# Attention block of a four-layer transformer stack: row maxima in four rows of the query stacks, and an attention output that stays by features

## The chip, the cores and the metric

The kernel runs on one core of one Trainium2 chip. The metric is the device time of one execution in microseconds, from its first to its last instruction and what lies around them. Several executions are taken and the median is given.

## The reference, cut to what matters

There are 16 sequences of 256 tokens with 256 features, each with a context of 77 tokens, and four layers:

```
L0: self-attention (rotary, masked), cross-attention, MLP   (each modulated and gated)
L1: cross-attention                                          (modulated)
L2: self-attention, cross-attention, MLP
L3: self-attention (rotary), cross-attention (rotary), MLP
```

An attention block is `softmax(q k^T / 4) v` with 16 heads of 16 features, a projection of the result, and a residual add. All of it is in float32. There are 16 x 7 = 112 attention blocks, 48 self and 64 cross, and 48 MLPs.

## The kernel before, in words

**Order of the work.** A job is one sequence in one layer, 64 jobs in all. Every block of a job is cut into steps (`attention_steps`), and each step belongs to one engine. A planner in Python (`Program.run`) goes through all jobs with the cost of every step (`cost`), the time its DMA takes on the queue (`ISSUE`) and rings of buffers, up to six jobs at a time in six slots. It writes down one fixed order for each engine. On the chip the engines follow their orders, and semaphores hold them where an input isn't there. So a step that comes later than planned holds all that stands behind it on its engine. SP's queue (SyncE) is such an order too: it issues nearly all the DMAs, and waits in front of each for its source.

**Scores.** A head has only 16 features. Queries and keys are split into a high and a low part, and a pair of heads takes a block of 64 rows of 128 partitions. `q_stack` and `k_self`/`k_cross` are filled by DMA through a scratch tensor in DRAM: features 1, 2 and 3 of every four partitions hold parts of the values (`place_high`, `place_low`, steps `lh`, `ll`). Every fourth partition (`0:P:4`, 32 rows) is spare. In the key stacks these rows hold ones or zeros (`hot`), so that what stands in the query stack's rows is added to the scores. The step `zq` (`place_zeros`) fills them with zeros. Then TensorE computes the scores by query (`S`), VectorE their maxima (`mr`, L1637), and `mx` (`negate_maximum`) negates and splits them and turns them in 32x32 blocks, four STREAM_TRANSPOSEs one after the other (L1656). `sd` (`place_maxima`, L1058) writes them by one DMA into all 32 rows of `q_stack`, for each half of the heads. `ST` then computes the scores by key (L1238, L1244) with the maximum already taken off, and ScalarE takes the exponential (`ex`, L1454).

**Output.** `W` (`weigh`, L1263) multiplies values by probabilities. A head's value tile is 17 columns wide, 16 features and a column of ones for the sum of the row. Four heads go side by side into four groups of 32 partitions, two such groups of heads into one bank. `pv` (ScalarE, L1461) copies the bank to `oT`. `oX` (`transpose_back`, L1274) turns it to tokens by four TensorE transposes, `dv` (`divide`, L1665 and L1666) divides by the sums, `atT` (`transpose_output`, L1285) turns it back by four (in a self block two and two), `ae` (L1466) copies it to `atT`, and `out` (`project_out`, through L1146) projects it. `oX`, `dv` and `pv` come once per half of the heads, 224 times.

```
for c in range(TC):
    for i in range(PER_HALF):
        at_col = (c * PER_HALF + i) * P
        mm = pe.transpose(buf[:, at_col:at_col + P], oT[before.buf][:, i, c * P:c * P + P], ident[:, :])
```

## Time and profile before

| | |
|---|---|
| time, median of 3 | 2863.39 us (2859.39 to 2871.44) |
| profiled execution, span | 2855.2 us, 57728 instructions |
| profiled execution, its own time | not listed; a timed execution is 4 to 16 us over this span |
| DMA | 369.43 MB in 278894 packets, mean 129 GB/s |

The span runs from the first to the last instruction of one execution that the hardware profiler recorded. A busy TensorE is not one at its peak: matmuls are pipelined and their ends are modelled. An engine's idle time costs something only where the engine sets the pace. PE is TensorE's matmul, PEld its weight load, DVE is VectorE, ACT ScalarE, POOL GpSimd, SP SyncE; a q behind the name is the engine's DMA queue. L1274 is line 1274 of the kernel. The rows that the prediction uses stand further down.

### The profile page before, as it was taken

What the parts mean: (1) busy time and instruction counts of PE and PEld (TensorE: products, weight loads), DVE (VectorE), ACT (ScalarE), POOL (GpSimd) and SP (SyncE); (2) the same over time, 40 slices, a digit from 0 to 9 for tenths busy, and PEclk for the clock granted to TensorE, in tenths of its full rate; (3) what the DMA queues carried; (4) which work ended last, traced back from release to release, by engine and by line L of the source; (5) the groups of instructions that cost most, each with busy time, mean ns of one, the idle gap of its engine ahead of it and who ended that gap; (6) DMA issues with size and microseconds to landing.
All of it is one profiled execution on the core that took longest, in us unless ns stands there. A gap on an engine that the chain in (4) does not pass through costs nothing.

```text
span 2855.2 us, 57728 instructions
## 1 busy us (share of the span) xinstructions
PE 2716.6 (95%) x21118; PEld 2000.2 (70%) x21118; DVE 1990.0 (70%) x5348; ACT 1433.3 (50%) x2283; POOL 290.6 (10%) x346
## 2 busy tenths in 40 slices
PE   6989999999998999988999999999999999999998
PEld 5657777776766766665777777776777777676766
DVE  4677757766755577776777777776877777787751
ACT  1344554554455455444555555545555555555453
POOL 0000000000001111101111111110100000000000
PEclk9999999999999999997999999999999999999999
DMA  6443343343335366653434444434344433434320
GB/s 199 154 137 116 117 141 106 99 145 109 104 95 149 115 198 191 196 163 122 155 122 139 126 141 125 141 121 131 104 141 138 139 112 107 146 103 145 101 69 14
DMA packets 278894, 369.43 MB, mean 129 GB/s; under 512 B 31130, under 2 KB 157690, under 8 KB 278300
## 3 DMA queue, kind: packets, MB, share of 16 engines
q1 hardware_dynamic: 246172, 318.66, 36.8%
q10 hardware_dynamic: 32256, 47.07, 4.5%
q8 instruction: 177, 2.90, 0.4%
q14 instruction: 97, 0.79, 0.1%
q0 software_dynamic: 192, 0.01, 0.0%
HBM read 224.52 MB, written 110.97 MB: 118 GB/s over the span
## 4 chain that ended last, share of the span: by engine, by line
PE 70%; DVE 16%; issue 5%; DMA 4%; ACT 1%; SPq 1%; POOL 0%; ACTq 0%; DVEq 0%; POOLq 0%
PE gen L1305 11%; PE gen L1314 11%; PE gen L1180 10%; PE gen L1146 8%; PE gen L1263 8%; DVE row_max L1637 6%; PE score L1238 3%; PE score L1193 3%; PE score L1208 3%; PE score L1244 2%; PE gen L1274 2%; PE gen L1155 2%; PE score L1222 2%; DMA parts_scratch<-parts 2%; DVE maxT L1656 2%
## 5 line engine op out<-in xcount | busy, mean ns | idle before, releaser
L1637 DVE TENSOR_REDUCE row_max<-score 128x4 f32<-128x1024 f32 (+1 forms) x640 | 652.6, 1044 | 107.9 <-PE score L1222 88.2
L1454 ACT ACTIVATE probs<-score 128x1024 f32<-128x1024 f32 (+1 forms) x576 | 566.2, 1022 | 268.2 <-PE score L1238 170.3
L1305 PE MATMUL gen<-xnT,w_w1M 128*128 128x256 f32 x1536 | 378.4, 394 | 4.7 <-ACT xnT L1396 2.6
L1314 PE MATMUL gen<-w_w2M,hT 128*128 128x256 f32 x1536 | 354.8, 385 | 8.6 <-DVE x L1688 5.7
L1490 POOL TENSOR_TENSOR rstd<-var_eps,minus_half 128x2 f32<-128x2 f32 x160 | 111.5, 697 | 2175.1 <-DVE var_eps L1533 2175.1
L1314 PEld LDWEIGHTS gen<-w_w2M,hT 128*128 128x128 f32 x1536 | 286.2, 191 | 59.2 <-issue 22.3
L1305 PEld LDWEIGHTS gen<-xnT,w_w1M 128*128 128x128 f32 x1536 | 286.1, 194 | 58.8 <-issue 4.9
L1480 ACT ACTIVATE hT<-gen,b_b 128x256 f32<-128x256 f32 x384 | 160.2, 471 | 166.6 <-PE gen L1305 165.7
L1396 ACT ACTIVATE xnT<-gen,mod_all 128x256 f32<-128x256 f32 x288 | 147.0, 564 | 181.0 <-PE gen L1155 164.4
L1656 DVE STREAM_TRANSPOSE maxT<-max_tok 32x64 f32<-32x64 f32 x896 | 208.9, 233 | 17.1
L1461 ACT COPY oT<-gen 128x512 f32<-128x512 f32 x224 | 131.6, 587 | 171.4 <-PE gen L1263 168.9
L1208 PE MATMUL score<-k_self,q_stack 64*128 64x256 f32 x1536 | 195.7, 343 | 19.7 <-DVE row_max L1637 17.3
L1263 PE MATMUL gen<-probs,v_self 128*17 128x256 f32 x3072 | 201.8, 383 | 0.3 <-ACT probs L1454 0.3
L1686 DVE TENSOR_TENSOR xhat<-gen,gate 128x256 f32<-128x256 f32 (+1 forms) x112 | 60.2, 537 | 203.2 <-PE gen L1314 147.8
L1208 PEld LDWEIGHTS score<-k_self,q_stack 64*128 64x128 f32 x1536 | 128.1, 190 | 95.9 <-issue 77.0
L1238 PE MATMUL score<-q_stack,k_self 64*128 64x256 f32 x1536 | 181.2, 334 | 2.9 <-ACT probs L1454 2.2
L1222 PEld LDWEIGHTS score<-k_cross,q_stack 64*128 64x128 f32 x2048 | 137.5, 192 | 50.6 <-issue 49.5
L1238 PEld LDWEIGHTS score<-q_stack,k_self 64*128 64x128 f32 x1536 | 122.1, 188 | 64.5 <-issue 46.0
L1222 PE MATMUL score<-k_cross,q_stack 64*128 64x78 f32 x2048 | 156.3, 284 | 9.1 <-DVE row_max L1637 5.8
L1263 PE MATMUL gen<-probs,v_cross 77*17 77x256 f32 x2048 | 159.7, 402 | 4.9 <-DVE xhat L1666 1.9
L1665 DVE RECIPROCAL row_max<-gen 128x16 f32<-128x16 f32 x224 | 55.0, 246 | 133.1 <-PE gen L1274 132.9
L1274 PE MATMUL gen<-ident,oT 128*128 128x128 f32 x896 | 143.2, 284 | 0.0
(162 smaller groups left out, 4166.4 us busy)
## 6 DMA issues: line engine op xcount, KB each, us to landing
q_stack<-parts_scratch SPq DMA_DIRECT2D x336, 256.0 KB, 3.8
parts_scratch<-parts ACTq DMA_DIRECT2D x160, 256.0 KB, 2.6
parts_scratch<-parts SPq DMA_DIRECT2D x160, 256.0 KB, 2.9
k_self<-parts_scratch SPq DMA_DIRECT2D x144, 256.0 KB, 4.0
q_stack<-zeros_scratch SPq DMA_DIRECT2D x112, 256.0 KB, 3.9
q_stack<-maxT SPq DMA_DIRECT2D x224, 128.0 KB, 2.6
k_cross<-parts_scratch SPq DMA_DIRECT2D x192, 78.0 KB, 2.5
x_scratch<-x SPq DMA_DIRECT2D x48, 256.0 KB, 3.1
```

The costliest lines, as they stand in the source:

```text
L1146: mm = pe.matmul(out, xT[:, fc], weight[:, fc, cols], start=fc == 0, stop=fc == FC - 1)
L1180: mm = pe.matmul(out[:, c, :], weight[:, fc, cols], xT[:, fc, :], start=fc == 0, stop=fc == FC - 1)
L1208: mm = pe.matmul(buf[:, t, c * S:c * S + S], queries[rows, column(u), c * P:c * P + P], keys[rows, column(u), :], start=not blk.mask, stop ...
L1222: mm = pe.matmul(buf[:, t, at_col:at_col + CTXP], queries[rows, column(2 * u + i), c * P:c * P + P], keys[rows, column(2 * u + i), :], sta ...
L1238: mm = pe.matmul(buf[:, t, kc * S:kc * S + S], keys[rows, column(u), kc * P:kc * P + P], queries[rows, column(u), :], start=not blk.mask, ...
L1263: mm = pe.matmul(pv[VW * i:VW * i + VC, within, :], value, e, start=kc == 0, stop=not blk.whole or kc == TC - 1, skip_group_check=True)
L1274: mm = pe.transpose(buf[:, at_col:at_col + P], oT[before.buf][:, i, c * P:c * P + P], ident[:, :])
L1305: mm = pe.matmul(buf[:, i * S:i * S + S], w["M"]["w1"][:, fc, col:col + P], xnT[s][:, fc, :], start=fc == 0, stop=fc == FC - 1)
L1314: mm = pe.matmul(buf[:, 0:D], hT[:, j, c * P:c * P + P], w["M"]["w2"][:, j, :], start=j == 0, stop=j == FFC - 1)
L1454: act.activation(probs[st.probs][0:keys, :, :], score[st.fill.buf][0:keys, :, :].rearrange("p a (r q) -> p (a r) q", r=2), ACT.Exp, bias=k ...
L1637: dve.tensor_reduce(dst, src, AX_X, ALU.max).then_inc(max_done[b], 1)
L1656: ins = dve.transpose(maxT[st.got["max"]][:, :, 32 * b:32 * b + 32].bitcast(F32), max_tok[st.got["max"]][32 * b:32 * b + 32, :, :].bitcast ...
```

## The change

Two things are changed together, and the planner's costs with them.

**Maxima.** The four parts (high and low of two heads) stand in four rows, 0, 32, 64 and 96, of the query stacks, in place of 32. `hot` in the key stacks is changed to match. `zq` fills 32 rows for the first use of each buffer and 4 after that. `mx` turns with one STREAM_TRANSPOSE of 128 partitions. A new step `sm` on SP stores the turned maxima in DRAM, and `sd` loads them from there into the four rows.

**Output.** The values of two heads are interleaved in one tile of 34 columns with ones at both ends, so `ve` has two instructions (one for each head of the pair) where it had one. `W` reads 32 columns, 0 to 31 or 2 to 33, and so leaves one head's features in the odd rows and the other's in the even rows. `pv` copies the bank to `oT` and its second group to `atT` as well. `sg` gathers the sums by two DMAs, `sh` lays the first group's odd rows into `atT` by one DMA, both on SP. `dv` inverts the sums once per block and spreads them over the features, `nm` multiplies, and `out` follows. `oX`, `atT` and `ae` are gone. The rows of the output weights are loaded in the new order (two DMAs in place of one).

```diff
-VC = HD + 1
+VC = 2 * HD + 2
...
-ISSUE = {"ldw": 2.5, "la": 0.5, "ms": 0.4, "zq": 0.63, "lh": 1.26, "ll": 0.63, "sd": 0.63}
+ISSUE = {"ldw": 2.5, "la": 0.5, "ms": 0.4, "zq": 0.4, "lh": 1.26, "ll": 0.63, "sg": 0.86, "sm": 0.4, "sd": 0.4}
...
-            "mx": 0.92,
-            "ST": 0.34 + 0.43 * mask if whole else 0.3, "ex": 0.92, "W": 0.99 if whole else 0.56, "pv": 0.48,
-            "oX": 0.44, "dv": 0.63, "atT": 0.22 if whole else 0.44, "ae": 0.26 if whole else 0.48, "out": 1.73,
+            "mx": 0.45,
+            "ST": 0.34 + 0.43 * mask if whole else 0.3, "ex": 0.92, "W": 0.99 if whole else 0.56, "pv": 0.85,
+            "sg": 2.0, "sh": 2.1, "dv": 1.35, "nm": 0.63, "out": 1.73,
...
-            "ldx": 2.8, "ldc": 2.2, "ldg": 4.0, "stx": 2.2, "zq": 3.6, "sd": 3.0, "ldw": 9.0,
+            "ldx": 2.8, "ldc": 2.2, "ldg": 4.0, "stx": 2.2, "zq": 2.2, "sm": 2.2, "sd": 2.2, "ldw": 9.0,
...
-            spread = [add("sd", h, "sp", [mx])]
+            spread = [add("sd", h, "sp", [add("sm", h, "sp", [mx])])]
...
             pv = add("pv", h, "act", sums, sums[0])
-            oX = add("oX", h, "pe", [pv])
-            divided.append(add("dv", h, "dve", [oX], oX))
...
+            gathered.append(add("sg", h, "sp", [pv]))
+            placed.append(add("sh", h, "sp", [pv]))
+        scaled = add("nm", 0, "dve", [add("dv", 0, "dve", gathered)] + placed)
+        out = add("out", 0, "pe", [scaled])
...
+                    step = 4 if before is None else 32
+                    src = zeros_dram.unsqueeze(1).to_broadcast([1, PAIRS // FC, FC * S])[0].partition_broadcast(P // step)
+                    sp.dma_start(rows_of(st)[0:P:step], src).then_inc(parts_placed[0][st.slot], 16)
...
+                def store_maxima(st):
+                    s, h = st.slot, st.j
+                    sp.wait_ge(max_turned, of(st, "mx", h).nth_all)
+                    if st.nth_part > 1:
+                        sp.wait_ge(rows_ready[h][s], 16 * 2 * (st.nth_part - 1))
+                    sp.dma_start(max_dram[s, h].rearrange("r (c b i) -> b r c i", c=TC, b=P // 32),
+                                 maxT[of(st, "mx", h).got["max"]][:, :, :].bitcast(F32)).then_inc(rows_ready[h][s], 16)
...
+                    sp.wait_ge(*maxima_stored(of(st, "sm", h)))
+                    src = max_dram[s, h].rearrange("(g n) k -> g n k", n=PAIRS)[:, h * pairs:(h + 1) * pairs]
+                    sp.dma_start(queries_of(st)[0:P:32, h:PAIRS:FC, :].bitcast(F32), src).then_inc(rows_ready[h][s], 16)
+
+                def place_sums(st):
+                    s, h, buf = st.slot, st.j, of(st, "pv", st.j).buf
+                    sp.wait_ge(*moved(of(st, "pv", h).fill))
+                    sp.dma_start(sums[s][2 * h + 1:P:VW, 0, :], oT[buf][0:P:VW, 0, :]).then_inc(sums_placed[buf], 16)
+                    sp.dma_start(sums[s][2 * h:P:VW, 0, :], oT[buf][VW - 1:P:VW, 1, :]).then_inc(sums_placed[buf], 16)
+
+                def place_heads(st):
+                    s, h, buf = st.slot, st.j, of(st, "pv", st.j).buf
+                    sp.wait_ge(*moved(of(st, "pv", h).fill))
+                    sp.dma_start(atT[s][1:P:2, h, :], oT[buf][1:P:2, 0, :]).then_inc(heads_placed[buf], 16)
...
-                            mm = pe.matmul(pv[VW * i:VW * i + VC, within, :], value, e, start=kc == 0,
+                            mm = pe.matmul(pv[VW * i:VW * i + VW, within, :], value, e, start=kc == 0,
...
-                        if st.prior["back"] is not None:
-                            act.wait_ge(*filled(st.prior["back"]))
+                        before = st.prior["back"]
+                        if before is not None:
+                            act.wait_ge(*sums_in(of(before, "sg", before.j)))
+                            act.wait_ge(*heads_in(of(before, "sh", before.j)))
                         pv = gen[st.fill.buf][:, :].rearrange("p (g t) -> p g t", g=PER_HALF)
-                        act.copy(oT[st.buf][:, :, :], pv).then_inc(gen_moved[st.fill.buf], 1)
+                        act.copy(oT[st.buf][:, :, :], pv)
+                        act.copy(atT[s][:, j, :], pv[:, 1, :]).then_inc(gen_moved[st.fill.buf], 1)
...
-                    for b in range(P // 32):
-                        ins = dve.transpose(maxT[st.got["max"]][:, :, 32 * b:32 * b + 32].bitcast(F32),
-                                            max_tok[st.got["max"]][32 * b:32 * b + 32, :, :].bitcast(F32))
-                    ins.then_inc(max_turned, 1)
+                    dve.transpose(maxT[st.got["max"]][:, :, :].bitcast(F32), max_tok[st.got["max"]][:, :, :].bitcast(F32)).then_inc(max_turned, 1)
+
+                def invert(st):
+                    s = st.slot
+                    for h in range(HALVES):
+                        dve.wait_ge(*sums_in(of(st, "sg", h)))
+                    link(dve.transpose(sums[s][:, 1, :], sums[s][:, 0, :]))
+                    total = rsum[s][:, :, :].rearrange("p c h -> p (c h)")
+                    link(dve.reciprocal(total.rearrange("p (h b e) -> p h b e", h=HALVES, e=2),
+                                        sums[s][:, 1, :].rearrange("p (b r) -> p b r", r=VW)[:, :, 0:2 * HALVES].rearrange("p b (h e) -> p h b e", e=2)))
+                    link(dve.transpose(inverse[s][:, :, :].rearrange("p c k -> p (c k)").rearrange("p (n d e) -> p n d e", d=HD, e=2),
+                                       total.rearrange("p (n e) -> p n e", e=2).unsqueeze(2).to_broadcast([P, HALVES * S // VW, HD, 2])))
...
+                    for h in range(HALVES):
+                        dve.wait_ge(*heads_in(of(st, "sh", h)))
+                    dve.tensor_tensor(atT[s][:, :, :], atT[s][:, :, :], inverse[s][:, :, :], ALU.mult).then_inc(divided, 1)
```

## Rows read from the trace of the kernel before

**Rows 1.** Busy time by stretch: us, busy PE, PEld, DVE, ACT, POOL, granted clock, DMA, GB/s.
```profile
0.00:215.00 215.00, 179.97 (x1344) 127.44 (x1345) 133.24 (x334) 65.70 (x99) 10.22 (x18) 0.94 0.52 163
215.00:860.00 645.00, 628.00 (x5159) 460.50 (x5157) 442.32 (x1114) 326.47 (x495) 49.46 (x61) 1.00 0.37 115
860.00:1360.00 500.00, 457.43 (x3551) 328.79 (x3550) 334.91 (x1038) 242.74 (x419) 71.00 (x83) 0.90 0.53 162
1360.00:1860.00 500.00, 498.49 (x3914) 373.17 (x3914) 368.64 (x1003) 276.72 (x452) 82.19 (x94) 1.00 0.45 137
1930.00:2700.00 770.00, 746.40 (x5781) 554.82 (x5780) 592.04 (x1540) 421.13 (x659) 56.50 (x67) 0.99 0.40 126
```
**Rows 2.** The chain that ended last, shares of the span by engine.
```profile
PE 70%; DVE 16%; issue 5%; DMA 4%; ACT 1%; SPq 1%; POOL 0%; ACTq 0%; DVEq 0%; POOLq 0%
```
**Rows 3.** TensorE in order of time: start us, us, what.
```profile
904.63 0.60 PE L1274 MATMUL gen<-ident,oT 128*128 128x128 f32 x4
905.07 1.89 PE L1180 MATMUL gen<-xnT,w_qB 128*128 128x256 f32 x8
906.80 0.60 PE L1285 MATMUL gen<-ident,xhat 128*128 128x128 f32 x4
907.33 0.31 PE L1215 MATMUL score<-kbias_row,pick 64*128 64x312 bf16 x2
```
**Rows 4.** Groups of TensorE instructions: busy us, mean ns of one, idle before.
```profile
L1274 PE MATMUL gen<-ident,oT 128*128 128x128 f32 x896 | 143.2, 284 | 0.0
L1285 PE MATMUL gen<-ident,xhat 128*128 128x128 f32 x448 | 81.1, 287 | 17.1 <-DVE xhat L1666 13.7 <-issue 2.4
L1238 PEld LDWEIGHTS score<-q_stack,k_self 64*128 64x128 f32 x1536 | 122.1, 188 | 64.5 <-issue 46.0
L1263 PEld LDWEIGHTS gen<-probs,v_self 128*17 128x17 f32 x3072 | 71.1, 97 | 63.1 <-issue 10.5 <-ACT probs L1454 0.2
L1263 PEld LDWEIGHTS gen<-probs,v_cross 77*17 77x17 f32 x2048 | 39.4, 97 | 54.9 <-issue 36.4 <-ACT probs L1454 2.9
```
**Rows 5.** One `W` pair of steps in order of time, loads and matmuls.
```profile
1506.97 0.56 PEld L1263 LDWEIGHTS gen<-probs,v_self 128*17 128x17 f32 x16 [0.33 <-issue]
1506.97 1.06 PE L1263 MATMUL gen<-probs,v_self 128*17 128x256 f32 x16
```
**Rows 6.** Groups of VectorE instructions, shapes apart.
```profile
L1656 DVE STREAM_TRANSPOSE maxT<-max_tok 32x64 f32<-32x64 f32 x896 | 208.9, 233 | 17.1
L1666 DVE TENSOR_TENSOR xhat<-gen,row_max 128x256 f32<-128x256 f32 x224 | 95.1, 425 | 7.7
L1665 DVE RECIPROCAL row_max<-gen 128x16 f32<-128x16 f32 x224 | 55.0, 246 | 133.1 <-PE gen L1274 132.9
L1569 DVE STREAM_SHUFFLE parts<-gen 128x512 f32<-128x512 f32 x80 | 58.6, 732 | 0.4
L1574 DVE TENSOR_TENSOR turned<-turned,parts 128x512 f32<-128x512 f32 x80 | 55.4, 692 | 2.8
```
**Rows 7.** Groups of ScalarE instructions, shapes apart.
```profile
L1461 ACT COPY oT<-gen 128x512 f32<-128x512 f32 x224 | 131.6, 587 | 171.4 <-PE gen L1263 168.9 <-ACT parts L1433 2.3
L1466 ACT COPY xnT<-gen 128x256 f32<-128x256 f32 x96 | 35.8, 373 | 63.9 <-PE gen L1285 63.8
```
**Rows 8.** DMAs: queue's packets, MB, share of 16 engines; then issues, KB each, median us to landing.
```profile
q1 hardware_dynamic: 246172, 318.66, 36.8%
...
q_stack<-maxT SPq DMA_DIRECT2D x224, 128.0 KB, 2.6
...
gates_scratch<-gates SPq DMA_DIRECT2D x1, 48.0 KB, 1.7
```
**Rows 9.** Issue of DMAs on SP: ns min/median/max.
```profile
L1058 SPq DMA_DIRECT2D q_stack<-maxT x224: 607/612/747, 81.7 to 2797.0; - x112
L1020 SPq DMA_DIRECT2D parts_scratch<-parts x224: 319/334/1104, 55.3 to 2766.0; - x112
```
**Rows 10.** SP's queue in order of time, in L1: start us, us, what.
```profile
1077.71 2.58 SPq L1042 DMA_DIRECT2D q_stack<-parts_scratch  x2
```

More of the change, by code:

```diff
@@ L130, in cost @@
     if name == "ve" and not whole:
-        return 0.38
+        return 0.55
     if name == "res":
@@ L163, in rings_of @@
     takes, gives = (), ()
-    if name in ("xT", "cT", "qkv", "oX", "atT", "out", "up", "down", "md", "mg"):
+    if name in ("xT", "cT", "qkv", "out", "up", "down", "md", "mg"):
         takes += ("gen",)
-    if name in ("xe", "ce", "ve", "rt", "dv", "ae", "res", "ge", "ma", "mh") or name == "lo" and not blk.rope:
+    if name in ("xe", "ce", "ve", "rt", "res", "ge", "ma", "mh") or name == "lo" and not blk.rope:
         gives += ("gen",)
@@ L499, in run @@
                 st.nth_way = seen[st.name, st.slot, "way", st.j, st.blk.whole or st.j == 0]
-def chunks_of(blk, h):
-    return [h] if blk.whole else list(range(FC))
 def column(n):
@@ L844, in dit_stack @@
         q_stack = [sb(f"q_stack{i}", [P, PAIRS, S], F32R) for i in range(QUERIES)]
-        maxT = [sb(f"maxT{i}", [4 * PAIRS, TC, P], F32R) for i in range(MAXIMA)]
+        maxT = [sb(f"maxT{i}", [P, TC, 4 * PAIRS], F32R) for i in range(MAXIMA)]
         row_max = per_slot("row_max", [P, TC, H])
@@ L870, in dit_stack @@
         rows_ready = [slot_sems(f"rows_ready{h}_") for h in range(HALVES)]
+        sums_placed, heads_placed = ([sem(f"{n}{i}") for i in range(BACKS)] for n in ("sums_placed", "heads_placed"))
+        divided = sem("divided")
         biased = sem("biased")
@@ L1288, in project_out @@
                 def project_out(st):
                     s, blk = st.slot, st.blk
-                    for h in range(HALVES if blk.whole else 1):
-                        pe.wait_ge(*moved(of(st, "atT", h)))
+                    pe.wait_ge(divided, of(st, "nm").nth_all)
                     buf = fill(st)
```

130 lines of the change are left out of this document (57 added, 73 removed).

## The prediction

> **What bounds the kernel now.** I read the busy time by stretch first, since an average over four layers hides what sets the pace in each. In three stretches TensorE is busy 97 to 100% of the time: 628.00 of 645 us (most of L0), 498.49 of 500 (L2) and 746.40 of 770 (L3) [rows 1]. VectorE has 69, 74 and 77% there, ScalarE 51 to 55%. Together they are 1915 us, 67% of the span. In what is left TensorE waits more: 457.43 of 500 us around L1, where the granted clock is 0.90 and the DMA share 0.53, and 179.97 of 215 at the start [rows 1]. The chain that ended last, read second, agrees with reservations: 70% PE, but 16% VectorE, 5% issue and 4% DMA [rows 2]. So TensorE's queue is the bound for two thirds of the span, and a mixture of VectorE, latency and DMA for the rest. A saving on TensorE counts in full in the first part only; elsewhere it meets VectorE's work or a landing DMA.
>
> **TensorE, removed.** `oX` and `atT` go. A busy time of 284 ns for one transpose is no cost, since they overlap, so I take the distance from a step's start to the next step's: 905.07 - 904.63 = 0.44 us for the four of `oX`, 907.33 - 906.80 = 0.53 us for the four of `atT`, where the array also changes its tile shape [rows 3]. 896 transposes are 224 steps of `oX`, 448 make the equal of 112 full steps of `atT` [rows 4]: 224 x 0.44 + 112 x 0.53 = 98.6 + 59.4 = 158 us. From below it is 336 x 0.44 = 148, from above, by the 0.60 us that four last including their tail [rows 3], 202. I take 158, since TensorE's queue is full and only distances count there.
>
> **TensorE, added.** The weight loads of `W` get 32 columns in place of 17, 3072 + 2048 = 5120 of them [rows 4]. The rows have 97 ns at 17 columns and 188 at 128: 0.82 ns a column, so 15 columns are 12.3 ns each and 63 us in all if nothing hides them. Nothing is the other end: 16 loads take 0.56 us beside 1.06 us of matmuls [rows 5]; scaled by the columns they would take 0.56 x 32 / 17 = 1.05, still inside. A gain is excluded, a wider load isn't faster. I take +10, near the lower end, because the next load runs beside the matmul before it.
>
> The Trainium skill speaks against that cover. "TensorE: Matmul & The Clock Gate", section "LDWEIGHTS (loading the stationary operand)", gives columns / 1.2 ns, and its section "The mechanism" says a load overlaps matmuls in flight only where the row group differs; here four column tiles share their rows. The slope in the rows agrees with the first (0.82 against 0.83 ns). By the second the sum would lose nearly the whole 63 us, but the trace's 0.56 us of loads beside 1.06 us of matmuls speaks against it.
>
> **VectorE.** `mx` has one transpose where it had four. The row is of 32 partitions and 64 elements in each. I take the time to go by the elements of a partition, so that one over 128 partitions costs 233 ns again (at worst 4 x 233, and nothing is saved): 3 x 233 x 224 = 157 us go [rows 6]. The old `dv` goes too: 55.0 + 95.1 = 150 us [rows 6]. New per block: a transpose of 256 elements (between the 233 ns at 64 and the 732 ns of a shuffle of 512, 1.11 ns an element: 0.45 us), a reciprocal of 32 (246 ns at 16, so 0.25 to 0.49; 0.35), a transpose of 512 (0.73), `nm` over 512 (0.69), and three waits between them, some 0.1 us. That is 2.32 us, 260 us for 112 blocks, 230 to 290 with the bounds. `ve` with bias: 64 more instructions; one of 256 elements costs 425 ns, a small one 246 [rows 6], so a split costs 0.07 to 0.25 us more, +10. Net: -157 - 150 + 260 + 10 = -37 us of 1990. In L3 VectorE has 592.04 of 770 us, 77%; with two attention blocks fewer by 0.5 us each in a period that shrinks 5% it goes to about 79%. No new bound, but it is what is late next. Since VectorE is 16% of the chain [rows 2], 37 us less is worth some 6.
>
> **ScalarE.** `pv` copies half a bank more: 224 x 0.373 = +84 us. `ae` goes: 96 x 0.373 + 64 x 0.587 = -73 [rows 7]. `ve` splits in L0 and L3 cost about +12 by the same rows. ScalarE stays near 52%, hidden under TensorE. New is that `pv` waits for the three DMAs that read the `oT` buffer of two halves ago. Behind it stand the exponentials that TensorE waits for. A half comes every 2855 / 224 = 12.7 us, so the buffer is wanted back some 25 us later, against landings of 2 to 3 us, and I cost this at nothing; uncovered, it is up to 2 us each time.
>
> **DMA and SP's queue.** Bytes fall: per half the 128 KB of the maxima become 32 stored and 16 loaded, zeros shrink from 256 to 32 KB a block, 64 KB of heads come in. Packets rise: a half's store is 256 runs of 128 bytes, 57,000 in all, and at the queue's own mean (36.8% of 16 engines for 246172 packets, 68 ns each [rows 8]) they cost 7% of the engines at most, about what leaves. No change here. SP issues four more DMAs per half (`sm`, two of `sg`, one of `sh`), between 0.33 and 0.61 us each [rows 9]: 1.3 to 2.4 us a half, 300 to 540 us in all, 10 to 19% of the span. In the saturated stretches that is free. In L1 two issues took 2.58 us where two need 1.2 [rows 10], so the queue is already backed up, and `sg` waits there for `pv` with the next job's loads behind it. For that reason I give L1 little of the gain.
>
> **Latency.** The maxima reach TensorE by two landings in place of one of 2.6 us. The lowest row to DRAM is 1.7 [rows 8], so 3.4 to 5.2 plus one more issue: +1.4 to +3.2 us a half; I take 2.4. The output path trades two trips through TensorE and a copy (0.44 + 0.67 + 0.53 + 0.37 us and their hops) for a gather of about 2.6 with its issue and 2.32 of VectorE: +2 to +3. With six jobs in flight this hides behind other jobs' matmuls in the 1915 us. It shows at the end, where the last job is alone: two blocks x 5 us = 10.
>
> **The sum.** In the saturated stretches 67% of 158 = 106 us. Of the other 52 I count half, 26. Then -10 for loads, -10 for the end, +6 for VectorE: 118 us. The profiled span of 2855.2 becomes 2737. The median of the runs shown lies 8 us over that span (what lies around the span and run-to-run spread), so the time is 2745, 4.1% less.
>
> **The rivals.**
>
> *Full gain.* All 158 us count, loads are hidden, lighter DMAs help L1 and VectorE's saving goes through: 158 + 15 = 173, so 2690. For it: 92% busy TensorE even around L1. Against it: the chain's 25% of VectorE, issue and DMA [rows 2].
>
> *Half the gain.* The loads cost most of their 63 us, or L1 loses on SP's queue what it gains on TensorE: 158 - 26 - 63 - 10 = 59, so 2804; down to 30, 2833. For it: the slope of the loads and the backed-up queue [rows 4, 10]. Against it: the loads' 0.56 beside 1.06 us [rows 5].
>
> *Slower: the row maxima come late.* TensorE follows a fixed order, written with 2.2 us for `sm` and 2.2 for `sd`. If the two landings take longer, the first `ST` of each half stands at the head of TensorE's queue and everything behind it waits. It decides from 118 / 224 = 0.53 us of uncovered wait per half; at 1 us the time is 2863 + 224 - 118 = 2969. For it: two landings at the present 2.6 miss the plan by 0.8 us, and the store is many runs of 128 bytes. Against it: where TensorE's queue is full it reaches `ST` late itself, and the lateness of the DMA is covered up to that amount.
>
> "DMA: Bandwidth & Descriptors", in its section on why a DMA increments its semaphore by 16, gives the Trainium skill's reason for such a miss: the number of DMA engines divides the slowest dimension of both sides, which is 4 in the destination of `sm` and `sd`. By that rule 64 runs stand on each of four engines. At the queue's 68 ns a packet that is 4.4 us, for a landing of about 6 instead of 2.2; no row of before shows a DMA of this shape.
>
> *It does not do what it says*: VectorE or SP becomes the pace and the time doesn't move, 2850 to 2875. In L3 VectorE would have to go from 77 to over 95%, which nothing in the sum does.
>
> **How the numbers follow.** Forecast (2700 to 2795) 0.56; full gain 0.12; half the gain 0.18; no change 0.04; slower 0.10. The range 2685 to 2830 takes in the forecast, most of the full gain and most of the half, and leaves out about 0.17. A change under 0.5%, 14 us, can't be told from none. Faster by more: 0.85; within: 0.05; slower: 0.10.
>
> **What would show it.** Right: TensorE's busy time falls by about 224 us (143.2 + 81.1), STREAM_TRANSPOSE of `maxT` has 224 instructions of 233 ns, L2 is still saturated and its period is 5 to 6% shorter, the loads of L1263 average near 110 ns with an unchanged distance between `W` steps. Wrong: a `W` pair that takes 1.2 us or more from start to next start; TensorE idle ahead of L1238 and L1244, released by a DMA into `q_stack`; ScalarE idle ahead of `pv`, released by a DMA; a stretch of L1 longer than before with SP always issuing.

## The result, and the profile after

The changed kernel takes 2903.36 us (median of 4, 2890.60 to 2913.47), the kernel before 2862.75 us beside it: a ratio of 1.0131, 95% interval [1.0095, 1.0168]. It is 40 us slower where 118 us less was forecast, and outside the range of 2685 to 2830. Two of the runs below had one execution far above their others (4992 us with all three costs out, 3061 us for the maxima part nudged); their times are medians of the other executions.

First the head of the page after: span, busy time of each engine, and the chain that ended last.

```profile
span 2894.5 us, 55650 instructions
...
PE 2672.0 (92%) x19774; PEld 1925.7 (67%) x19774; DVE 1924.2 (66%) x4739; ACT 1517.0 (52%) x2483; POOL 296.4 (10%) x346
...
PE 45%; DVE 24%; issue 9%; ACT 8%; DMA 7%; SPq 5%; POOL 0%; ACTq 0%; DVEq 0%; POOLq 0%
```

TensorE's busy time fell by only 44.6 us (from 2716.6), where the prediction named 224. The transposes are gone, but they had overlapped with other work, and what stayed takes longer: matmuls of unchanged shape average 355 ns (L1253) and 299 ns (L1267) where they had 343 and 284, at a lower granted clock. The chain went from 70% PE to 45%, with VectorE at 24% in place of 16% [rows 2]. The same stretches as [rows 1] of the kernel after (us, then busy PE, PEld, DVE, ACT, POOL, granted clock, DMA share, GB/s):

```profile
0.00:215.00 215.00, 169.84 (x1240) 119.69 (x1240) 120.62 (x284) 62.52 (x103) 10.60 (x18) 0.90 0.47 145
215.00:860.00 645.00, 607.92 (x4884) 437.26 (x4884) 432.24 (x977) 337.58 (x540) 50.38 (x60) 0.98 0.35 110
860.00:1360.00 500.00, 454.50 (x3335) 323.30 (x3334) 325.27 (x930) 254.45 (x453) 72.45 (x84) 0.86 0.48 146
1360.00:1860.00 500.00, 471.92 (x3509) 341.61 (x3508) 342.01 (x866) 275.37 (x453) 79.59 (x90) 0.96 0.39 123
1930.00:2700.00 770.00, 722.22 (x5145) 518.94 (x5146) 555.82 (x1312) 451.36 (x711) 59.85 (x68) 0.93 0.35 112
```

The stretch of L2, which had 498.49 of 500 us busy with 3914 matmuls at clock 1.00, now has 471.92 with 3509 at 0.96. L3 goes from 0.99 to 0.93. So every stretch that was called saturated has gaps now, and the clock that TensorE is granted is lower in all five. (The windows are fixed in time, so they don't hold quite the same work in both kernels.)

What the engines of the kernel after wait for (total us, times, longest), VectorE's first, then SP's queue and TensorE:

```profile
DVE xhat L1684 <- DMA xhat<-oT: 179.6, 57, 12.9
```

```profile
SPq L1092 <- ACT xnT L1486: 269.6, 96, 10.2
SPq L1087 <- DMA max_scratch<-maxT: 172.0, 137, 3.2
```

```profile
PE score L1238 <- DMA q_stack<-max_scratch: 7.9, 5, 3.1
...
PE score L1289 <- DMA q_stack<-max_scratch: 3.6, 6, 1.2
```

The largest single wait of VectorE is new: the first transpose of `dv` waits 57 times for the gathered sums, 180 us in all. `sd` waits at most 3.2 us for the stored maxima (L1087), and TensorE waits 11.5 us in the whole run for them (7.9 + 3.6; before it was 6.8). The groups that answer to [rows 4, 6, 7], shapes apart (busy us, mean ns, idle before):

```profile
L1688 DVE STREAM_TRANSPOSE xhat<-row_max 128x512 f32<-128x512 f32 x112 | 79.7, 711 | 3.9
L1695 DVE TENSOR_TENSOR xnT<-xnT,xhat 128x512 f32<-128x512 f32 x112 | 79.5, 713 | 1.7 <-DMA xnT<-oT 0.9
...
L1677 DVE STREAM_TRANSPOSE maxT<-max_tok 128x64 f32<-128x64 f32 x224 | 55.0, 245 | 7.8
...
L1684 DVE STREAM_TRANSPOSE xhat<-xhat 128x256 f32<-128x256 f32 x112 | 49.0, 437 | 179.7 <-DMA xhat<-oT 179.6
...
L1686 DVE RECIPROCAL row_max<-xhat 128x32 f32<-128x32 f32 x112 | 39.5, 353 | 3.8
```

```profile
L1309 PEld LDWEIGHTS gen<-probs,v_self 128*32 128x32 f32 x3072 | 82.5, 110 | 65.4 <-issue 16.4
...
L1309 PEld LDWEIGHTS gen<-probs,v_cross 77*32 77x32 f32 x2048 | 46.2, 114 | 62.1 <-issue 41.2 <-ACT probs L1476 10.9
```

```profile
L1485 ACT COPY oT<-gen 128x512 f32<-128x512 f32 x224 | 131.7, 588 | 122.4 <-PE gen L1309 114.0 <-DMA xnT<-oT 5.1 <-ACT parts L1455 1.9
L1500 ACT ACT_TABLE_LOAD x88 | 112.9, 1283 | 44.6 <-PE gen L1329 43.2 <-ACT parts L1455 0.4
L1476 ACT ACT_TABLE_LOAD x87 | 111.6, 1283 | 4.4 <-ACT parts L1455 2.2 <-ACT parts L1468 0.7
L1486 ACT COPY xnT<-gen 128x256 f32<-128x256 f32 x224 | 86.9, 388 | 0.0
```

`mx` costs about what was said, 245 ns for each of 224 transposes against 233. The new block work of VectorE is 437 + 353 + 711 + 713 = 2214 ns against 2320 forecast. The 32-column loads average 110 and 114 ns, as forecast. Not forecast: ScalarE loads its activation table 175 times for the exponential and GELU in place of 103, 72 more of 1.283 us, because the planner's new order alternates between them more often. The two groups in the kernel before:

```profile
L1480 ACT ACT_TABLE_LOAD x52 | 66.7, 1283 | 151.1 <-PE gen L1305 151.0
L1454 ACT ACT_TABLE_LOAD x51 | 65.4, 1283 | 3.7 <-ACT parts L1433 2.9
```

One such wait of VectorE, in order of time in the kernel after (start us, us, what, idle before):

```profile
1744.05 1.07 PE L1309 MATMUL gen<-probs,v_self 128*32 128x256 f32 x16
...
1745.75 0.59 ACT L1485 COPY oT<-gen 128x512 f32<-128x512 f32 x1
1746.22 0.41 ACT L1486 COPY xnT<-gen 128x256 f32<-128x256 f32 x1
1746.65 0.55 SPq L1092 DMA_DIRECT2D xhat<-oT  x1
...
1748.93 0.45 DVE L1684 STREAM_TRANSPOSE xhat<-xhat 128x256 f32<-128x256 f32 x1 [4.35 <-DMA xhat<-oT]
```

`pv` ends at 1746.63, SP issues `sg` at once, and the sums are there 2.3 us later. VectorE has stood for 4.35 us by then, so about half of this wait is for `pv` itself and not for the gather. The landing is short, as forecast. But the chain `W`, `pv`, `sg`, `dv`, `nm` is in VectorE's fixed order, where `oX` and `atT` had it on TensorE, and everything that stands behind `dv` waits with it: maxima, key parts, the residual.

### The profile page after: what moved, and what is told of

Same layout as the page of the kernel before. It is cut to its first block, busy times and chain, and to the rows that moved or that the text cites. A ratio compares the mean times of both kernels' runs of the same rounds, so it can differ in the third digit from the quotient of the medians.

```text
span 2894.5 us, 55650 instructions
## 1 busy us (share of the span) xinstructions
PE 2672.0 (92%) x19774; PEld 1925.7 (67%) x19774; DVE 1924.2 (66%) x4739; ACT 1517.0 (52%) x2483; POOL 296.4 (10%) x346
## 3 DMA queue, kind: packets, MB, share of 16 engines
q1 hardware_dynamic: 284860, 292.06, 32.9%
## 4 chain that ended last, share of the span: by engine, by line
PE 45%; DVE 24%; issue 9%; ACT 8%; DMA 7%; SPq 5%; POOL 0%; ACTq 0%; DVEq 0%; POOLq 0%
DVE row_max L1659 10%; PE gen L1329 8%; PE gen L1338 8%; PE gen L1225 7%; PE gen L1309 6%; PE gen L1191 4%; ACT probs L1476 3%; PE score L1283 3%; DMA xhat<-oT 2%; PE gen L1200 2%; PE score L1267 2%; DMA parts_scratch<-parts 2%; DVE stats L1547 2%; PE score L1238 2%; SPq L1061 2%
## 5 line engine op out<-in xcount | busy, mean ns | idle before, releaser
L1329 PE MATMUL gen<-xnT,w_w1M 128*128 128x256 f32 x1536 | 367.1, 391 | 5.9 <-DVE v_cross L1637 3.3
L1338 PE MATMUL gen<-w_w2M,hT 128*128 128x256 f32 x1536 | 363.3, 392 | 2.7 <-ACT hT L1500 2.4
L1253 PE MATMUL score<-k_self,q_stack 64*128 64x256 f32 x1536 | 203.8, 355 | 31.7 <-DVE row_max L1659 23.6
L1253 PEld LDWEIGHTS score<-k_self,q_stack 64*128 64x128 f32 x1536 | 135.2, 201 | 114.0 <-issue 95.5
L1309 PE MATMUL gen<-probs,v_self 128*32 128x256 f32 x3072 | 208.1, 390 | 1.3 <-ACT probs L1476 1.0
L1283 PE MATMUL score<-q_stack,k_self 64*128 64x256 f32 x1536 | 193.5, 347 | 10.4 <-DVE row_max L1659 5.0
L1309 PE MATMUL gen<-probs,v_cross 77*32 77x256 f32 x2048 | 180.1, 434 | 11.8 <-DVE x L1716 4.4
L1267 PEld LDWEIGHTS score<-k_cross,q_stack 64*128 64x128 f32 x2048 | 146.4, 205 | 60.9 <-issue 60.4
L1267 PE MATMUL score<-k_cross,q_stack 64*128 64x78 f32 x2048 | 165.7, 299 | 16.7 <-DVE row_max L1659 12.1
L1684 DVE STREAM_TRANSPOSE xhat<-xhat 128x256 f32<-128x256 f32 x112 | 49.0, 437 | 179.7 <-DMA xhat<-oT 179.6
L1714 DVE TENSOR_TENSOR xhat<-gen,gate 128x512 f32<-128x512 f32 (+1 forms) x112 | 59.7, 533 | 140.8 <-PE gen L1338 120.3
L1466 ACT ACTIVATE parts<-gen,b_qk 128x256 fp32r<-128x256 f32 (+1 forms) x192 | 71.1, 425 | 155.2 <-PE gen L1225 139.5
L1500 ACT ACT_TABLE_LOAD x88 | 112.9, 1283 | 44.6 <-PE gen L1329 43.2
```

What stands on the lines that cost most here:

```text
L1253: mm = pe.matmul(buf[:, t, c * S:c * S + S], queries[rows, column(u), c * P:c * P + P], keys[rows, column(u), :], start=not blk.mask, stop ...
L1267: mm = pe.matmul(buf[:, t, at_col:at_col + CTXP], queries[rows, column(2 * u + i), c * P:c * P + P], keys[rows, column(2 * u + i), :], sta ...
L1283: mm = pe.matmul(buf[:, t, kc * S:kc * S + S], keys[rows, column(u), kc * P:kc * P + P], queries[rows, column(u), :], start=not blk.mask, ...
L1309: mm = pe.matmul(pv[VW * i:VW * i + VW, within, :], value, e, start=kc == 0, stop=not blk.whole or kc == TC - 1, skip_group_check=True)
L1329: mm = pe.matmul(buf[:, i * S:i * S + S], w["M"]["w1"][:, fc, col:col + P], xnT[s][:, fc, :], start=fc == 0, stop=fc == FC - 1)
L1338: mm = pe.matmul(buf[:, 0:D], hT[:, j, c * P:c * P + P], w["M"]["w2"][:, j, :], start=j == 0, stop=j == FFC - 1)
```

## The experiments

All were run in rounds beside the kernel before; each ratio is to it.

**The parts alone.** The first holds the maxima part only, the second the output part only, each with the planner's costs that belong to it.

```diff
# e1: before, with hot, zq, mx, sm, sd and their costs changed
+                    dve.transpose(maxT[st.got["max"]][:, :, :].bitcast(F32), max_tok[st.got["max"]][:, :, :].bitcast(F32)).then_inc(max_turned, 1)
# e2: before, with VC = 34, ve, W, pv, sg, sh, dv, nm and the rows of the output weights changed
-                            mm = pe.matmul(pv[VW * i:VW * i + VC, within, :], value, e, start=kc == 0,
+                            mm = pe.matmul(pv[VW * i:VW * i + VW, within, :], value, e, start=kc == 0,
```

> The kernel before with the maxima part alone: four rows of the query stacks, one turn on VectorE, a store and a load through DRAM, and the planner's costs of that part; the output path with its TensorE transposes stays. Theory A (the output part is to blame: VectorE waits in its fixed order for the gathered sums): this part alone is neutral or a gain, 2840 to 2870 us. Rival B (the maxima come late by two landings): most of the loss is here, 2880 us or more. Rival C (any new order of the steps costs some per cent by chance of the plan): anything from 2830 to 2900, with no wait that stands out.

> The changed kernel with the maxima part undone: 32 rows by one DMA from SBUF, four turns. Theory A: slower than before by itself, 2890 to 2930 us, with VectorE idle over 150 us in front of the turn of the sums. Rival B: 2770 to 2850, since the removed transposes pay once the maxima are on time. Rival C: unclear.

Measured: maxima alone 2813.04 us, ratio 0.9817 [0.9794, 0.9841]; output alone 3010.40 us, 1.0506 [1.0483, 1.0529]. The heads of their pages, the engines' busy time and the chain, maxima alone first:

```profile
PE 2689.5 (96%) x21118; PEld 1989.2 (71%) x21118; DVE 1820.7 (65%) x4675; ACT 1442.7 (51%) x2293; POOL 291.4 (10%) x346
...
PE 73%; DVE 12%; DMA 6%; issue 3%; ACT 3%; SPq 2%; POOL 0%; ACTq 0%; DVEq 0%; POOLq 0%
```

```profile
PE 2728.8 (91%) x19774; PEld 1967.0 (65%) x19774; DVE 2090.8 (69%) x5412; ACT 1501.2 (50%) x2469; POOL 294.7 (10%) x346
...
PE 51%; DVE 27%; issue 7%; DMA 5%; ACT 5%; SPq 3%; POOL 0%; ACTq 0%; DVEq 0%; POOLq 0%
```

In these orders the whole loss is the output part's: alone it costs 144 us, more than either rival had said, and the maxima part alone gains more than any had. With the maxima part alone the chain is 73% PE and VectorE's busy time falls by 169 us. With the output part alone VectorE has 2090.8 us, 101 more than before, and the clock is 0.914. VectorE waits 126.3 us for the sums there, less than the 179.6 of the changed kernel, although the time is longer. So this wait isn't the measure of the loss. That the maxima part brings more beside the output part (107 us, 3010 to 2903) than alone (53) fits with what it takes off VectorE, but each kernel has its own order, and no run separates the two.

**Costs of the output part, taken out one by one from the changed kernel.** No gather: the two DMAs of `sg` and the waits for them are gone (the inversion reads stale sums). Free inversion: no gather, and `dv` waits for nothing in its place. Light inversion: the reciprocal and the spreading transpose are left out of `dv`, so the result is not divided rightly. One table: the GELU is an identity, in the changed kernel and in the kernel before.

```diff
# e6 (no gather); e7 leaves the last wait out as well
-                    sp.dma_start(sums[s][2 * h + 1:P:VW, 0, :], oT[buf][0:P:VW, 0, :]).then_inc(sums_placed[buf], 16)
-                    sp.dma_start(sums[s][2 * h:P:VW, 0, :], oT[buf][VW - 1:P:VW, 1, :]).then_inc(sums_placed[buf], 16)
-                        dve.wait_ge(*sums_in(of(st, "sg", h)))
+                        dve.wait_ge(*moved(of(st, "pv", h).fill))
# e14
-                    link(dve.reciprocal(...))
-                    link(dve.transpose(inverse...))
# e4, and e5 in the kernel before
-                        fn = ACT.Gelu_apprx_tanh if blk.gelu == "tanh" else ACT.Gelu
+                        fn = ACT.Identity
```

> The changed kernel, same planned order, without the two DMAs of sg: VectorE inverts what happens to stand in its tile (the sums are left out), as soon as both copies of pv are done. If the landing and issue of the gather (2.3 us or more) are what holds VectorE, its wait ahead of the turn of the sums (180 us) falls below 80 us and the time to 2830 or less. If the output itself (pv, W, the exponentials before it) comes late in the order, the wait stays over 120 us, now released by ScalarE, and the time stays above 2870.

> As the one before, and the inversion on VectorE waits for nothing (sums left out); only the product that follows waits for the heads. The 180 us of waiting move to the product or vanish. If VectorE standing in its fixed order in front of the inversion is the cause of the loss, 2820 us or less; if the wait only moves to the product (same lateness, 2 us further on), within 20 us of the run without the gather.

> The changed kernel without the reciprocal and the spreading transpose of the inversion (the output is left undivided by its sums): 112 x (0.35 + 0.71 + two waits) = 125 us of VectorE less, all waits and DMAs as they are. If VectorE's added work is what holds TensorE, 2840 or less; if it is hidden (VectorE is 66% busy), 2885 or more.

> The changed kernel with the GELU of the MLP replaced by Identity (the MLP's activation is left out), so that ScalarE loads no tables between exponentials and GELUs; the order of all steps is the same. The changed kernel has 175 table loads of 1.28 us where the one before had 103. If the 72 more loads (92 us of ScalarE) hold up TensorE, this falls by 60 us or more, to below 2845; if ScalarE's time is covered, by less than 20 us.

> The kernel before with the GELU of the MLP replaced by Identity (the activation is left out), so without the 102 table loads between exponential and GELU. With the changed kernel this gave 20 us for 174 loads. If loads cost in proportion, 12 us here and the more frequent switching accounts for some 8 us of the loss; if they cost nothing in a full TensorE queue, 0 here and the switching accounts for up to 20.

| left out | us | ratio to before | against 2903 |
|---|---|---|---|
| gather | 2858.58 | 0.9988 [0.9967, 1.0008] | -45 |
| gather and every wait of `dv` | 2860.48 | 0.9999 [0.9980, 1.0019] | -43 |
| reciprocal, spreading transpose | 2877.68 | 1.0054 [1.0033, 1.0076] | -26 |
| table loads, changed kernel | 2883.96 | 1.0072 [1.0046, 1.0098] | -19 |
| table loads, kernel before | 2860.88 | 0.9983 [0.9967, 0.9999] | (-4 against 2865.15 beside it) |

The gather is the largest, but 45 us is a quarter of the 180 us that were waited for it. VectorE's waits in the run without the gather show where the rest goes:

```profile
DVE xhat L1681 <- ACT xnT L1483: 56.1, 14, 10.5
...
DVE xnT L1692 <- DMA xnT<-oT: 25.1, 26, 2.6
```

VectorE now stands at the same transpose for `pv` itself (L1681) and at `nm` for the heads (L1692, 0.9 us before this edit), and its waits for the MLP's output (120.3 to 143.1 us) and for one group of scores (82.9 to 96.7) grow too. Without any wait of `dv` the time doesn't fall further, and the wait of `nm` grows to 68.4 us: the next wait in the chain takes its place. Table loads cost the changed kernel 17 to 19 us (by the ratios, by the medians), the kernel before 4 to 5. So some 12 to 15 us of the loss are the extra switches of ScalarE, which the prediction didn't have; the intervals of the four ratios leave anything from nothing to twice that.

**All three together.** The edits of e6, e14 and e4 in one kernel.

> The changed kernel with three of its costs taken out together: the landing of the weighted sums comes from no DMA (the scatter and gather of the sums are left out, so the output is not the attention's), the inversion of the sums has no reciprocal and no spreading transpose, and the GELU is an identity, so ScalarE loads no table. Alone they gave 45, 26 and 20 us. If each is a cost of its own, the time is 2903 - 91 = 2812 us, below the kernel before. If they are three views of one lost overlap, the best of them stands for all and the time is 2840 us or more. The rival, that the granted clock takes back what idle time is removed, wants a clock no higher than 0.94 and a time above 2840.

Measured: 2827.23 us, 0.9885 [0.9819, 0.995], which is 76 us under the changed kernel by the medians and 70 by the ratios; span 2825.1 us, clock 0.94. Far more than the best alone (45), and a little less than the sum (91 by the medians, 80 by the ratios): the three are in the main costs of their own, and an overlap is hardly clear of the interval. The rival of the clock wanted a time above 2840 and isn't borne out. Even with the three gone this kernel isn't faster than the maxima part alone (ratio 0.9817, the intervals touch), though it has 1344 transposes less on TensorE. What takes that saving too is not shown by a run.

**What TensorE's transposes were worth.** The other way round: the first puts as many transposes into the changed kernel as it lost (four dummy ones at each old place, results overwritten). The second takes 960 of the 1344 out of the kernel before and leaves all else as it is: one of four of `oX`, one in each `atT` (the output is then not the attention's).

```diff
# e8: changed kernel, at each pv's bank and ahead of out
+                        for i in range(4):
+                            pe.transpose(gen[first.buf][:, i * P:i * P + P], ident[:, :], ident[:, :])
# e13: kernel before
-                    for c in range(TC):
-                        for i in range(PER_HALF):
+                    for c in range(TC - 1, TC):
+                        for i in range(PER_HALF - 1, PER_HALF):
```

> The changed kernel with four transposes of the identity on TensorE ahead of each first W step of a half and ahead of each projection, 1344 as the change removed, into banks that are overwritten at once. If TensorE's queue were still the bound, this costs 150 us (3050). If the saving lies in time in which TensorE waits for VectorE anyway, under 60 us (below 2960). If the lower granted clock (0.936 against 0.973) is an effect of the idle time, the clock rises above 0.945 here and takes part of the cost back.

> The kernel before, same order and same steps, with one TensorE transpose left in each step of oX and atT: 384 of 1344 stay (the attention output is left wrong), 960 go, 71% of the forecast's 158 us, 113 us. If TensorE's queue is the bound and its time counts in full, 2750 to 2775. If the rest of the loop (VectorE, ScalarE, the fixed order) takes over, or the granted clock falls below its 0.973 and gives the time back, 2800 or more; the clock-corrected span (span times clock) then tells the two apart: it falls by 100 us or more if the clock does it, by less than 60 if the other engines do.

Measured: the filler costs 60 us (2963.24, 1.036 [1.0323, 1.0397]) of the 158 that its transposes are priced at, with 121 us more busy TensorE and a clock of 0.957 in place of 0.936. The kernel before with 71% of its transposes gone, 113 us by the prediction's prices, takes 2843.93 us, 0.9951 [0.9926, 0.9975]: 14 us less by the ratio (7 to 21 by its interval), 17 by the difference from the 2861.23 beside it. This is the run that decides. The same period of L2 in both kernels shows where the rest stays. TensorE in the kernel before (start us, us, what):

```profile
1505.08 1.97 PE L1180 MATMUL gen<-xnT,w_qA 128*128 128x256 f32 x8
...
1514.12 0.66 PE L1274 MATMUL gen<-ident,oT 128*128 128x128 f32 x4
1514.61 1.01 PE L1180 MATMUL gen<-ctxT,w_kvB 128*128 128x77 f32 x8
1515.56 1.13 PE L1222 MATMUL score<-k_cross,q_stack 64*128 64x78 f32 x16
1516.62 1.06 PE L1263 MATMUL gen<-probs,v_self 128*17 128x256 f32 x16
...
1551.81 0.66 PE L1285 MATMUL gen<-ident,xhat 128*128 128x128 f32 x4
1552.30 0.30 PE L1166 MATMUL gen<-ident,ctx_in 77*128 77x77 f32 x2
1552.46 0.89 PE L1180 MATMUL gen<-xnT,w_qA 128*128 128x256 f32 x3
```

The same places in the kernel with fewer transposes:

```profile
1497.29 1.97 PE L1180 MATMUL gen<-xnT,w_qA 128*128 128x256 f32 x8 [0.40 <-DVE parts L1598]
...
1506.34 0.33 PE L1274 MATMUL gen<-ident,oT 128*128 128x128 f32 x1
1506.51 1.01 PE L1180 MATMUL gen<-ctxT,w_kvB 128*128 128x77 f32 x8
1507.45 0.64 PE L1222 MATMUL score<-k_cross,q_stack 64*128 64x78 f32 x8
1508.26 0.64 PE L1222 MATMUL score<-k_cross,q_stack 64*128 64x78 f32 x8 [0.16 <-ACT probs L1454]
1508.82 1.06 PE L1263 MATMUL gen<-probs,v_self 128*17 128x256 f32 x16
...
1543.28 0.33 PE L1285 MATMUL gen<-ident,xhat 128*128 128x128 f32 x1
1543.44 0.30 PE L1166 MATMUL gen<-ident,ctx_in 77*128 77x77 f32 x2
1544.15 1.10 PE L1180 MATMUL gen<-xnT,w_qA 128*128 128x256 f32 x4 [0.41 <-DVE parts L1598]
```

The step of `oX` takes 0.17 us in place of 0.49, as it should, and over the four `oX` and three `atT` steps of the period TensorE's queue is relieved by 1.31 + 0.49 = 1.80 us. Yet the period goes from 1552.46 - 1505.08 = 47.38 us to 1544.15 - 1497.29 = 46.86. The pair of L1222 steps now takes 1.37 us in place of 1.06, with a wait for ScalarE's exponential, and `w_qA` comes 0.71 us after the context's transposes in place of 0.16, with a wait for VectorE (`parts`). A pair of L1208 steps takes 0.96 us (1514.32 to 1515.28) in place of 0.68 (1522.48 to 1523.16). These three places hold 1.14 us. TensorE was 99.7% busy here, and VectorE and ScalarE were a few tenths of a microsecond behind it at these points of the order. In this stretch both kernels have a granted clock of 1.00, as the row of L2 of this kernel shows (columns as above), so it is the other engines in their fixed orders, and not the clock, that hold back 1.28 of 1.80 us:

```profile
1360.00:1860.00 500.00, 491.74 (x3733) 359.03 (x3726) 376.39 (x1018) 279.76 (x459) 85.47 (x97) 1.00 0.44 137
```

The period is no exception. Followed from one TensorE instruction to the same one in the other trace, the work that took the kernel before 499.9 us in L2 takes 494.4: 5.6 us for 184 transposes, which this period's 1.80 us for 17 would put at 19.5. The same work in the kernel before with the GELU as an identity, in the same order, repeats within 0.1 us. Elsewhere the clock takes part too. From 400 to 860 us, 145 transposes are gone and the same work takes 461.6 us in place of 460.1, while its clock goes from 1.00 to 0.97. L1 has 0.88 against 0.90 in [rows 1], and over the span it is 0.958 against 0.973. The measure that was set beforehand, span times clock, falls by 58 us, just under the 60 that stood for the other engines and far from the 100 that stood for the clock.

**The planner's order.** A cost in the planner moves no work, but changes the written orders. Four orders of the changed kernel, and the maxima part and the kernel before with others of theirs:

```diff
# e3: changed kernel, costs as its trace has them (SP's issue times and sm too)
-            "mx": 0.45, ... "pv": 0.85, "sg": 2.0, "sh": 2.1, "dv": 1.35, "nm": 0.63,
+            "mx": 0.7, ... "pv": 0.97, "sg": 2.4, "sh": 2.6, "dv": 1.6, "nm": 0.7,
# e12: the same with "sg": 2.8, "sh": 3.0; e9: the same with 5.0 for both
# e10, e17: kernel before with "mx": 1.44 and 0.97 in place of 0.92
# e11, e15: maxima part alone with "mx": 0.7 (and sm, sd as measured) and 0.5 in place of 0.45
```

> The changed kernel with the planner's costs of the new steps set to what the trace after shows: mx 0.70 (was 0.45), dv 1.6 (1.35), nm 0.70 (0.63), sg 2.4 and sh 2.6 (2.0, 2.1), sm 2.4 (2.2), pv 0.97 (0.85), and SP's issue times 1.15, 0.52, 0.57, 0.53 for sg, sh, sm, sd. If the loss comes from an order written with wrong costs, VectorE's 180 us of waiting for the sums shrink to under 60 and the time falls below 2850. If the wait belongs to the longer path itself or to chance of the order, the time stays within 30 us of 2903.

> The run with measured costs, with 2.8 and 3.0 us for sg and sh in the planner in place of 2.4 and 2.6: a nudge that no mechanism speaks for. If the costs work through their being right, 2830 to 2850. If the order is to a large part chance, it lies anywhere from 2820 to 2890, and the 63 us between the changed kernel and the one with measured costs are no proof of a mechanism.

> The run with the measured costs, but with 5.0 us for sg and sh in the planner in place of 2.4 and 2.6, so that the inversion is placed later in VectorE's order. If the loss is VectorE standing before sums that are planned too early, the wait falls below 90 us and the time below 2825. If the longer path binds, the time rises above 2850.

> The kernel before, with nothing changed but the planner's cost of mx, 1.44 us as the trace of before shows it (it had 0.92). A control for what an order is worth by itself. If orders written with right costs are worth some 2% here as well, 2800 to 2830; if the gain of the maxima part (2813) came from its smaller work, this stays within 15 us of 2863.

> The kernel before with one figure of the planner (the step with the row maxima) raised from 0.92 to 0.97; no work is added or removed, only the order that the planner writes can differ. If the order is worth little to the kernel before, the time is within 10 us of 2863 us, and the 40 us by which the changed kernel is slower are the change's. If chance in the order is worth +-25 us here too, as between the orders of the changed kernel (2840 to 2903), it comes out at 2838 or 2888 us, and part of the verdict on the change is the chance of one order.

> The maxima part alone, with the measured costs in the planner (mx 0.70 in place of 0.45, sm 2.4, and SP's issue times 0.57 and 0.53). If right costs help here as they did with both parts (63 us), 2750 to 2795. If the effect of the costs is that of the output part's steps, within 20 us of 2813.

> The maxima part alone with 0.50 us for mx in the planner where it had 0.45 (2813) and 0.70 with three other costs (2867). If the part itself is worth 50 us and the order of the run with measured costs was unlucky, 2800 to 2825; if the 50 us are the luck of one order, 2840 to 2870.

| kernel | us | ratio to before |
|---|---|---|
| changed, costs measured (e3) | 2839.67 | 0.9916 [0.9889, 0.9942] |
| changed, nudged (e12) | 2856.24 | 0.9962 [0.9942, 0.9983] |
| changed, sums planned late (e9) | 2861.71 | 1.0001 [0.9977, 1.0025] |
| before, `mx` as measured (e10) | 2869.12 | 1.0017 [0.9999, 1.0035] |
| before, nudged (e17) | 2877.16 | 1.0036 [1.0016, 1.0056] |
| maxima alone, costs measured (e11) | 2867.33 | 1.0010 [0.9994, 1.0026] |
| maxima alone, nudged (e15) | 2832.56 | 0.9894 [0.9863, 0.9924] |

The order is worth as much as the change. The changed kernel lies between 2840 and 2903 us over four orders, the maxima part between 2813 and 2867 over three, the kernel before between 2863 and 2877 (0 to 0.4% by the ratios, over two small changes of one cost). The measured costs brought 64 us, but not by the way that was expected: VectorE's wait for the sums should have shrunk to under 60 us and is 164.3. Planning the sums late does remove this wait, as the run with measured costs and the one with late sums show:

```profile
DVE xhat L1684 <- DMA xhat<-oT: 164.3, 50, 17.0
```

```profile
DVE row_max L1659 <- PE score L1267: 163.7, 86, 12.2
DVE row_max L1659 <- PE score L1253: 120.2, 81, 16.6
...
DVE xhat L1684 <- DMA xhat<-oT: 29.4, 15, 5.9
```

From 164.3 to 29.4 us, and yet that kernel is slower than the one with measured costs (2862 against 2840): VectorE's waits for the scores are 284 us in place of 196.5 (125.8 + 70.7 in the other). The wait came back in another place.

## Why the prediction was wrong

**The failed step: "In the saturated stretches 67% of 158 = 106 us".** A TensorE that is 97 to 100% busy was taken for one whose every microsecond counts. The run with fewer transposes puts 113 us of this price at 14 to 17 us. In the period of L2 only 0.52 of 1.80 us is gained, and in the whole of L2 5.6 of 19.5, at a full clock. What the busy share doesn't show is how far the other engines are behind: they were a few tenths of a microsecond behind, and the chain's 30% of other engines and issue [rows 2], which the prediction read as a reservation for L1 and the start, held in L2 as well. In L0 and L1 the clock fell besides, for which the sum had no term; how much of the loss is the clock's there stays open. The sum's 106 + 26 = 132 us for TensorE become some 20 to 24 (158 x 14 / 113 and x 17 / 113, an estimate by proportion), or 60 by the filler in the changed kernel. Either way the output part had little to pay with.

**The price of the distances** (0.44 and 0.53 us a step) was nearly right: 0.32 or 0.33 us went with three of four transposes, of `oX` (0.33 by the price) and of `atT` (0.40) alike. What a step takes and what it is worth are two numbers.

**Weight loads, +10.** Right: 110 and 114 ns a load, and two `W` steps of eight loads each lie side by side in 1.07 us (the pair at 1744.05 above) where they had 1.06 [rows 5]. From the first `W` matmul of such a pair to the step behind it it is 1.00 us against 0.99 in the kernel before, the median of 192 pairs in each; 1.2 was named as the sign of being wrong. The slope is (110 - 97) / 15 = 0.87 ns a column. The rule of the Trainium skill weighed there ("TensorE: Matmul & The Clock Gate", section "The mechanism"), that such loads don't overlap with matmuls of the same rows, would make the pair 16 x 12.3 ns = 0.2 us longer; this is not seen.

**VectorE, -37 us of busy time, worth 6.** The work was priced well: its busy time fell by 65.8 us (1990.0 to 1924.2), in part because the new steps of a block came out shorter (2.21 us in place of 2.32, waits between them left out). Its worth was not. What a block does on VectorE in the middle of its fixed order costs more than its net sum says: without the reciprocal and one transpose, 1.06 us a block or 119 us in all, the kernel gains 26 us.

**ScalarE, hidden.** The copies were priced right (388 ns against 373), and `pv`'s new wait for its buffer, costed at nothing, is 5.1 us in all. 72 more table loads were not seen, as the prediction took the order for given. They cost some 12 to 15 us. To see them one would have had to run the planner, since no trace of before has the new order.

**DMA and SP's queue, no change.** Right in the main: the queue's share fell from 36.8 to 32.9% of the engines. (57,000 packets of 68 ns are 8.5% of them, not 7%.) SP now waits 270 us at L1092 for `pv` with the next job's loads behind it, as the prediction feared for L1, but it had waited 635 us at L1058 for the maxima before, and no run shows that its queue costs time.

**"With six jobs in flight this hides behind other jobs' matmuls."** The second step that failed. The landings were right (2.3 us from `pv` to the sums), but they are not hidden in a fixed order: VectorE waits 180 us for the sums, and without the gather the time is 41 to 45 us less (by the ratios, by the medians).

**The rivals.** *Slower: the maxima come late* had the right sign and the wrong mechanism. TensorE waits 11.5 us for them in all, not 224, and the part alone is the fastest kernel of all. The estimate of about 6 us for the landing, from the four-engine rule of the Trainium skill ("DMA: Bandwidth & Descriptors", section "Why a DMA increments its semaphore by 16 and not by 1"), is far off: where SP stood waiting for the stored maxima, `sd` was issued a median of 2.4 us after the start of `sm`. *It does not do what it says* had the truer picture, that something else sets the pace, but expected a VectorE at 95%. It is at 66% of the span.

**How much is the order's luck.** The planner's costs changed too, and they were too low for `mx`, `pv`, `sg`, `sh`, `dv` and `nm`. With measured costs the changed kernel is 2840 us, 0.8% under the kernel before. That the too low costs are the reason for the slow order isn't shown: a nudge of two of them by 0.4 us, for which nothing speaks, took 17 us back. So "40 us slower" belongs to this order; over its four orders the change is worth -5 us on average (2865 against 2870 over the three of before), not -118. The sign of the idea itself stays open. That the output part costs against the maxima part alone (2813, 2833, 2867, mean 2838, against a mean of 2865) is likelier than not, and alone, in its one order, it was 144 us slower, more than any order moved a kernel here (64). But its size isn't settled. Settled in the given orders are the failed step and what the gather, the inversion and the table loads cost.

**The best version** is the maxima part alone in its first order: 2813.04 us, 1.8% under the kernel before and 3.1% under the changed one.

## What to carry to other kernels

A busy share of 100% says that an engine has work, not that it sets the pace; before a saving on it is counted in full, ask how far behind it the others are at each of its hand-overs, and take a part of the saving alone, in an otherwise unchanged order, to see what it brings. A stage that is moved from the engine with the longest queue into another engine's fixed order brings its waits with it, and these hold what stands behind. Where a planner writes the order, compare several orders of both kernels before a difference under 2% is given to the change.

## What the runs showed of the hardware

In most stretches the granted clock fell when gaps came into TensorE's work. It did not in L2 with fewer transposes, which has waits of 0.16 and 0.41 us in a period and stays at 1.00. Over the span it was 0.973 before (2716.6 us busy of 2855.2), 0.958 with fewer transposes (2661.4 of 2839.8), 0.936 after (2672.0 of 2894.5), and 0.957 after with the filler (2793.3 of 2959.7). With the transposes put back it was higher, 0.957 in place of 0.936. The busy share alone doesn't give it: L1 of the kernel after is 91% busy at 0.86, the start 79% busy at 0.90, and L3 94% busy at 0.93 beside L2 with 94% at 0.96. The trace has two levels, 1.2 and 2.4 GHz, so a mean of 0.86 is 28% of that stretch at the lower level. Taking span x (1 - clock) as the most that the clock can cost, it is 77 us before, 119 with fewer transposes and 185 after. That is an upper end, since TensorE is not always what is waited for; how much of the 108 us between the kernels is really the clock's, no run here separates. A table load of ScalarE takes 1.283 us each time, and 103 of them (132 us of ScalarE) cost the kernel before 4 to 5 us, while 175 (225 us) cost the changed one 17 to 19. The likely reason, which no run isolates, is that the exponentials are waited for more often there.
